# Two-layer graph network on one core: another order for the last two passes

## What is computed

```python
h = jnp.maximum(_layernorm(x), 0.0)
x = x + _L0_gnn_ref(h, adj, ...)   # 12 heads of 32
h = jnp.maximum(_layernorm(x), 0.0)
x = x + _L1_gnn_ref(h, ..., adj)   # 6 heads of 64
```

## Time and profile before

| | |
|---|---|
| runs | 962.27, 965.95, 966.61 us; median 965.95 |
| profiled execution | 964.57 us |
| its span, first to last instruction | 962.7 us |
| mean granted TensorE clock | 0.98 |
| PE busy | 915.3 us, 95% |
| DVE busy | 792.9 us, 82% |
| ACT busy | 608.3 us, 63% |
| POOL busy | 208.5 us, 22% |
| hardware DMA queue | 54.83 MB, 32.9% of 16 engines |

### The profile page before, as it was taken

How to read it: one execution, slowest core, us unless ns; L and a number is a source line. 1 busy time by engine, 2 the same in 40 slices (tenths; PEclk the granted TensorE clock), 3 DMA queues, 4 the chain that set the end, 5 groups by cost and what they waited for, 6 DMA issues and landing times.

```text
span 962.7 us, 24702 instructions
## 1 busy us (share of the span) xinstructions
PE 915.3 (95%) x9851; PEld 816.8 (85%) x9851; DVE 792.9 (82%) x1537; ACT 608.3 (63%) x1277; POOL 208.5 (22%) x273
## 2 busy tenths in 40 slices
PE   5689999999999999999999999999999999999696
PEld 5487988989798897989889797988989898898575
DVE  5878979888897988889798898979888897888814
ACT  5547658575775857577585757658575765856432
POOL 2205040130504014050401405040130504013010
PEclk9889999999999999999999999999999999999988
DMA  9403252151525216152521516252151525222102
GB/s 216 83 3 33 35 101 35 39 79 19 101 35 98 38 39 79 19 100 35 98 38 37 80 21 100 35 100 36 47 71 19 100 35 101 35 49 36 42 11 66
DMA packets 185077, 56.41 MB, mean 59 GB/s; under 512 B 166402, under 2 KB 184964, under 8 KB 184964
## 3 DMA queue, kind: packets, MB, share of 16 engines
q1 hardware_dynamic: 184964, 54.83, 32.9%
HBM read 17.07 MB, written 12.58 MB: 31 GB/s over the span
## 4 chain that ended last, share of the span: by engine, by line
issue 48%; PE 28%; POOL 14%; ACT 4%; DVE 4%; DMA 0%; POOLq 0%; ACTq 0%; DVEq 0%
POOL x_in L430 6%; PE ps L694 4%; PE ps L696 4%; PE ps L695 4%; POOL x_in L436 4%; PE ps L680 4%; ACT p L458 3%; PE ps L761 3%; POOL rstd L408 2%; PE ps L762 2%; PE ps L765 2%; PE ps L880 1%; PE ps L774 1%; PE ps L897 1%; PE ps L838 1%
## 5 line engine op out<-in xcount | busy, mean ns | idle before, releaser
L403 POOL TENSOR_SCALAR ve<-mv 128x4 f32<-128x4 f32 x32 | 7.5, 233 | 646.7 <-DVE mv L943 645.5
L430 POOL TENSOR_TENSOR x_in<-x_in,bf_row 128x384 f32<-128x384 f32 x64 | 85.5, 1370 | 42.8 <-ACT p L458 42.8
L1091 DVE COPY_PREDICATED_SCALAR z<-not_adj,masked 128x768 f32 x64 | 69.8, 1091 | 26.4 <-ACT z L549 26.4
L953 DVE TENSOR_TENSOR hT1l<-ps,hT1h 128x384 fp32r<-128x384 f32 x128 | 62.8, 550 | 23.2 <-ACT hT1h L463 22.4
L512 ACT ACTIVATE ps<-hb_all 128x384 f32<-128x384 f32 x56 | 27.8, 497 | 73.2 <-DVE x_in L1103 73.2
L530 ACT ACTIVATE QT<-ps,bq_col 128x512 f32<-128x512 f32 x48 | 33.0, 688 | 62.6 <-PE ps L765 62.6
L938 DVE BATCH_NORM_STATS2 stats<-x_in 128x6 f32<-128x384 f32 x128 | 64.7, 546 | 6.4 <-DMA x_in<-in_x_dram 6.0
L694 PE MATMUL ps<-W_hi,hT0h 128*128 128x384 f32 x192 | 65.6, 342 | 2.0 <-DVE hT0l L953 2.0
L694 PE MATMUL ps<-Wf_hi,hT1h 128*128 128x384 f32 x192 | 66.0, 344 | 0.6 <-DVE hT1l L953 0.5
L694 PE MATMUL ps<-Wv_hi,hT1h 128*128 128x384 f32 x192 | 66.5, 346 | 0.0
L436 POOL TENSOR_TENSOR x_in<-x_in,h 128x384 f32<-128x384 f32 x64 | 62.8, 1016 | 14.3 <-DVE Wf_lo L983 14.3
(11 more groups left out here) (133 smaller groups left out, 2693.0 us busy)
## 6 DMA issues: line engine op xcount, KB each, us to landing
x_in<-in_x_dram SPq DMA_DIRECT2D x16, 768.0 KB, 5.1
V<-v_tok SPq DMA_DIRECT2D x64, 192.0 KB, 5.8
V<-v_tok SPq DMA_DIRECT2D x128, 96.0 KB, 2.4
out_dram<-x_in SPq DMA_DIRECT2D x16, 768.0 KB, 3.6
x<-in_L_gnn_H_w_dram SPq DMA_DIRECT2D x1, 576.0 KB, 6.0
QT<-in_L_gnn_W_dram SPq DMA_DIRECT2D x3, 192.0 KB, 6.8
thT<-in_L_gnn_Wq_dram SPq DMA_DIRECT2D x1, 576.0 KB, 5.3
z<-in_L_gnn_Wk_dram SPq DMA_DIRECT2D x1, 576.0 KB, 6.3
```

Of the source, the lines that this page charges most:

```text
L430: pool.tensor_tensor(x_in[:, j % 3, t], x_in[:, j % 3, t], bf_row[:], ALU.add).then_inc(x2_biased, 1)
L953: return dve.tensor_tensor(to[:, :, toks], ps[:, job(name, t) % BANKS, 0:D].rearrange("p (c m) -> p c m", m=P), high[:, :, toks].bitcast(F ...
L1091: dve.copy_predicated(zu, not_adj[:, tiles].unsqueeze(2).broadcast_to((P, 2, PAIRS0, N)), masked0[:].unsqueeze(2).unsqueeze(3).broadcast_t ...
```

## The change

It touches passes 15 and 16 alone (`last` is 15, `groups` is 16); passes 0 to 14 issue what they did.

- *Pass 15, TensorE:* all four `attend0` come ahead of the turn of the second-layer probabilities. The output product of group 14 is made here for tiles 0 and 1 only.
- *Pass 15, VectorE:* `divide0(3)` and `close(0)` come ahead of all low parts; the low parts of tiles 2 and 3, two `add_out` and the mask come behind `row_sums`; there is no other `add_out`.
- *Pass 15, ScalarE:* the exponentials of the ELU are placed around the copies of the turned probabilities, and the high parts of group 14's attention come last. These high and low parts go to `hT0h` and `hT0l`, which no later group needs.
- *Pass 16, TensorE:* the output product of group 14 for tiles 2 and 3 stands between the last values product and the turn of the last probabilities; VectorE adds it ahead of the low parts of group 15's attention. ScalarE's split of the last normalised input waits for `values1_full` in place of `final_full`.
- *Rings:* passes 15 and 16 have lists of their own, of 64 and 32 entries, with gaps.
- *SP:* group 14 is stored in pass 16, behind the spreading loads, and group 15 in four DMAs, one for a tile.

```diff
+        def gap(n):
+            return [("gap", groups + 2, None, 0, k) for k in range(n)]
+
+        last = groups - 1
+        to_scores = [entry[0] for entry in RING].index("probs0T_copied")
+        rings = {it: RING for it in range(NEXT, last)}
+        rings[last] = (
+            RING[0:to_scores]
+            + jobs("probs0T_copied", 0, probs0T_copied, 6)
+            + jobs("attn0_made", 0, attn0_made, 4)
+            + jobs("probs1T_copied", 1, probs1T_copied, 3)
+            + jobs("attn1_low", 1, attn1_low, 4)
+            + jobs("out_made", 1, out_made, 4)[0:2]
+            + gap(6)
+        )
+        rings[groups] = (
+            jobs("h1_low", 1, h1_low, 4)
+            + jobs("q_copied", 1, q_copied, 3)
+            + jobs("k_copied", 1, k_copied, 3)
+            + values1_jobs[0:2]
+            + jobs("scores1_shifted", 1, scores1_shifted, 4)
+            + values1_jobs[2:4]
+            + jobs("out_made", 2, out_made, 4)[2:4]
+            + jobs("probs1T_copied", 1, probs1T_copied, 3)
+            + jobs("attn1_low", 1, attn1_low, 4)
+            + jobs("out_made", 1, out_made, 4)
+            + gap(1)
+        )
...
-                if real(j):
+                if real(j) and j < last - 1:
                     sp.wait_ge(out_made, (j + 1) * TILES)
                     sp.dma_start(out_v[j], x_in[:, j % 3]).then_inc(out_stored, 16)
...
+                if j == last:
+                    sp.wait_ge(out_made, last * TILES)
+                    sp.dma_start(out_v[last - 1], x_in[:, (last - 1) % 3]).then_inc(out_stored, 16)
+                    for t in range(TILES):
+                        sp.wait_ge(out_made, last * TILES + t + 1)
+                        sp.dma_start(out_v[last, :, t], x_in[:, last % 3, t]).then_inc(out_stored, 16)
...
+                if i == last:
+                    exp_elu(0)
+                    exp_elu(1)
+                    copy_probs1()
+                    exp_elu(2)
+                    exp_elu(3)
+                    act.wait_ge(gate_full, TILES * groups)
+                    attn1_parts(hT0h)
...
                 attend0(0)
                 attend0(1)
...
+                if i == last:
+                    attend0(2)
+                    attend0(3)
+                    turn_probs1()
                     attend1(0)
                     attend1(1)
...
+                    output(j, (hT0h, hT0l), (0, 1))
+                else:
+                    if i == groups:
+                        output(j - 1, (hT0h, hT0l), (2, 3))
+                    turn_probs1()
+                    attend0(2)
...
+                if i == last:
+                    divide0(3)
+                    close(0)
+                    stats_of_x2(0)
+                    stats_of_x2(1)
+                    attn1_lows(hT0l, hT0h, (0, 1))
+                    close(1)
+                    stats_of_x2(2)
+                    stats_of_x2(3)
+                    row_sums(1, i)
+                    attn1_lows(hT0l, hT0h, (2, 3))
+                    add_out(0)
+                    add_out(1)
+                    make_mask1()
+                else:
+                    if i == groups:
+                        add_out(2, j - 1)
+                        add_out(3, j - 1)
+                    attn1_lows(hT1l, hT1h, range(TILES))
```

More of the change, by code:

```diff
@@ L269, in two_layer_gnn, with job, last_reader @@
         )
[L270 to L274, removed]
+        def gap(n):
[25 more added lines that the diff above has]
+        )
+        assert all(len(ring) % BANKS == 0 for ring in rings.values())
+        place = {(name, it - layer, k): (it, at)
+                 for it, ring in rings.items() for at, (name, layer, _, _, k) in enumerate(ring)}
+        def job(name, g, k):
+            return place[name, g, k][1]
         def hw_bank(c):
-            taken = [job("th_made", t) % BANKS for t in range(TILES - 1)] + [job("h0_low", k) % BANKS for k in range(TILES)]
+            taken = [job("th_made", 0, t) % BANKS for t in range(TILES - 1)] + [job("h0_low", 0, k) % BANKS for k in range(TILES)]
             return [b for b in range(BANKS) if b not in taken][c - C]
-        def last_reader(i, at):
-            it = i
+        def last_reader(name, g, k):
+            it, at = place[name, g, k]
             while True:
@@ L285, in last_reader @@
                 if at < 0:
[L286 to L289, removed]
+                    it -= 1
+                    if it < NEXT:
+                        return None
+                    at += len(rings[it])
+                name, layer, signal, n, k = rings[it][at]
                 if real(it - layer):
@@ L602, in body @@
                 if real(j):
-                    if real(j - 1):
+                    if j == last:
+                        act.wait_ge(values1_full, TILES * j)
+                    elif real(j - 1):
                         act.wait_ge(final_full, TILES * j)
@@ L861, in turn_probs @@
                     for q in range(jobs):
[L862 removed]
+                        take(name, n, q)
                         for k in range(4):
@@ L911, in body, with turn_probs1, output @@
                     turn_probs("probs0T_copied", probs0_made, unit_of, probs0_turned, lambda t: z[:, t], PAIRS0, i, 6)
+                def turn_probs1():
+                    if real(j):
+                        turn_probs("probs1T_copied", probs1_divided, pair_of, probs1_turned, p1_tile, PAIRS1, j, 3)
+                def output(g, parts, tiles):
+                    if real(g):
+                        for t in tiles:
+                            toks = slice(t * P, (t + 1) * P)
+                            take("out_made", g, t)
+                            pe.wait_ge(attn1_low, TILES * g + t + 1)
+                            product(ps[:, job("out_made", g, t) % BANKS, 0:D], lambda c: parts[0][:, c, toks], lambda c: parts[1][:, c, toks],
+                                    lambda c: wh["Wf"][:, c], lambda c: wl["Wf"][:, c]).then_inc(final_full, 1)
@@ L923, in body @@
-                if real(j):
-                    for t in range(TILES):
-                        toks = slice(t * P, (t + 1) * P)
-                        take(i, job("out_made", t))
-                        pe.wait_ge(attn1_low, TILES * j + t + 1)
-                        product(ps[:, job("out_made", t) % BANKS, 0:D], lambda c: hT1h[:, c, toks], lambda c: hT1l[:, c, toks],
-                                lambda c: wh["Wf"][:, c], lambda c: wl["Wf"][:, c]).then_inc(final_full, 1)
+                    output(j, (hT0h, hT0l), (0, 1))
[4 more added lines that the diff above has]
+                    attend0(2)
+                    if real(j):
+                        attend1(0)
+                        attend1(1)
+                    attend0(3)
+                    if real(i + 1):
+                        turn_h0(i + 1, 1 - par, range(TILES))
+                    output(j, (hT1h, hT1l), range(TILES))
```

226 lines of the change are left out of this document (113 added, 113 removed).

## The result

The changed kernel takes 959.14 us (median of 10 runs, 951.65 to 963.74); the kernel before, in runs beside it, 965.84. The ratio is 0.9926, 95% interval 0.9906 to 0.9946: 0.74% faster, some 7 us. The forecast was 958.5: gains of 6.8 us, taken off a level half-way between the profiled execution (964.57) and the median (965.95).

The account below looks back on a forecast made before the run. TensorE is busy 95% of the middle; the change targets its idle time in the last 65 us. Terms 3.79 + 0 + 1.41 + 1.60 = 6.80 off 964.57 give 957.8, plus half of 1.38: 958.5 us, range 955.5 to 961.8.

Parts of the forecast that it names:

- Term 1: VectorE in pass 15: last group's statistics aggregated 13.21 us after the first division, at 907.43 instead of 911.22; gain 3.79 us.
- Term 2: Start of pass 16: TensorE's clock low again at the first turn; gain taken as 0, ends 2.5 gain and 0.9 loss.
- Term 3: Last softmax: two tiles of group 14's product fill TensorE's wait and keep the clock high; gain 1.41 us, from 0.47.
- The clock's part: Last softmax and attention: at the high clock the first high part comes at 949.01; gain 0.94 us.
- The bank's part: Last output product: its bank in the new ring is freed long before, by a group 14 addition; gain 0.47 us.
- Term 4: Closing store by tiles: issue to end 2.35 us instead of 3.95; gain 1.60 us, ends 0 and 2.1.
- third rival: Pass 15: late ScalarE work or bank-freeing additions cost half to all of the 3.79 us; 960.4 to 962.3; chance 0.12.
- No saving by the quarter store: Closing store: a quarter costs what the whole does, so the 1.60 us is lost; 960.1 us; chance 0.12.
- stores in a row: Kernel end: the four stores run one after the other, each as long as the whole; about 966 us; chance 0.04.
- The clock falling anyway around the softmax: Last softmax: three short gaps bring the clock down all the same, losing 0.94 us; 959.4 us; chance 0.10.
- the new wait in pass 15: Pass 15: ScalarE's copies and exponentials or bank-freeing additions come late; 960.4 to 962.3 us; chance 0.12.
- The slow case: Pass 16: the clock falls at about 904 and doesn't rise in the projections; 969.3 us; chance 0.04.

Follow-up runs that it names:

- e1: The kernel before, with the last group alone stored by tiles; ratio 0.9988 to the kernel before.
- e3: The kernel before, with 18 matmuls on constant weights between the last values product and the turn of the last probabilities; ratio 1.0001.
- e2: The changed kernel with its last group stored in one DMA again; ratio 0.9934 to the kernel before.
- e5: The changed kernel with group 14's two filler tiles ahead of the last values products and their additions ahead of VectorE's last softmax; 962.53 us.
- e8: The changed kernel with 34 matmuls on constants in TensorE's idle stretch of pass 0, none in pass 15; 953.93 us.
- e10: The changed kernel with constant matmuls in the idle stretches of passes 0 and 15, and 12 more ahead of pass 0's score blocks; 953.76 us.
- e4: The changed kernel with VectorE's old order in pass 15 put back; ratio 0.9965 to the kernel before.

## Why the prediction was right

- **Term 1, VectorE's order (3.79):** 3.80. The sum of starts, 13.21 us from the first division to the aggregation, was met to within 0.02 in ten profiles of eight kernels. Against e1 and e3, in the old order, the gain would be 4.04: they took 17.24, not 17.00. No margin broke, though the product of the first two tiles took 4.8 us for the 3.2 reckoned, since the clock fell in it. What it had not counted: 0.12 us more from aggregation to turn.
- **Term 2, the clock at the start of pass 16 (0, from -0.9 to 2.5):** the first trace gave 2.5, the whole upper end; but over nine profiles the segment wanders between 21.0 and 23.7 in either order, so no share of the kernel's own can be told, and that 0 was right is not shown. Its premise, a low clock at the first projection, failed in both profiles of the changed kernel and held in e2, e5, e8 and e10. Nor did 1.9 us of idling bring the clock down as a rule: before 914.50 it fell 4.5 us into the idle stretch, in the changed kernel 1.5 us behind the end of one of 3.25.
- **Term 3, the filler (1.41):** 1.33. The clock's part was 0.96 for 0.94, shown apart by e3 and e5. The bank's part was sized 0.47 and is 0.37: the product now starts 0.14 us behind the end of the first low part.
- **Term 4, tiles (1.60):** 1.65. The fixed part, 1.75 of 3.95 us, stayed, within 0.2 us, and about a quarter of the moving part is left (0.6 us of 2.2).
- **Sum:** 6.70 in segments for 6.80; 959.14 us for 958.5, with a ratio whose interval is 5.2 to 9.1 us. Against the median of before alone the sum would have given 959.15, so the half-way level moved the forecast 0.6 away; in a spread of 951.65 to 963.74 that tells nothing. The upper bound, 961.8, is a point inside the third rival's 960.4 to 962.3, not an end of it.
- **Rivals.** No saving by the quarter store and stores in a row fell to e1. The clock falling anyway around the softmax, and the new wait in pass 15, fell to the rows above. The slow case, a clock that stays low through pass 16, never came: it rose at the latest 9.4 us behind the first turn (e1), and the longest low stretch lasted 17 us (907.5 to 924.5, e4).
- What the prediction had no idea of is how far one execution wanders: by 12 us over the ten of the changed kernel, and by 7 us over nine profiles in passes that the change doesn't touch. Its range was made of the clock and a microsecond or two; that it held is owed in part to the median of ten runs, which evens this out. A forecast judged by one profiled span would have missed by 6.

## What to carry to other kernels

At the end of a pipeline, ask which results the last group waits for, and let everything that only earlier groups wait for stand behind it on each engine; then put real work of an earlier group where the engine would idle, since that kept its clock up here as well (1.00 for 0.50 over the last attention, 0.96 us), and split the last store so that only one piece is behind the last result (1.65 us here). Sum from start to start along one engine, it was good to 0.02 us in ten profiles here; compare two traces in segments, never by their spans. Before a gain of under 1% is believed, put the same number of idle instructions elsewhere as a control (34 of them took some 4 us off here), and see in the trace where the blocks of instructions are fetched (a pass with a late fetch took 0.7 us more here).

## What was not expected of the hardware

- TensorE's clock at the start of pass 16 came up anywhere from the first projection (after 3.4 us) to 9.4 us behind the first turn, worth up to 2.8 us. Two executions of one kernel differ in it too: in pass 0 of the changed kernel's two profiles the clock rose 3.0 us behind the first turn in one and 4.3 in the other. 43 matmuls on constants hold it at 1.00 in all four profiles that have them.
- 34 instructions of no use at the start of TensorE's list made the kernel some 4 us faster (954.18 for 958.36 on the same chip, ratios 0.9878 and 0.9909) and took all idle rows without a releaser out of the fourteen middle passes: each block of instructions was then fetched 2.6 to 3.2 us ahead of the second attention, and no longer, in some passes, less than 0.75 us. Whether the changed kernel's own gain holds a part of this stays open; its segments say that 6.7 us need none.
- The last 192 KB store took 2.3 us from issue to the end of the span (the changed kernel), the last 768 KB store 3.95 (the kernel before).
